# A GIN pass whose selection matrices move to GpSimd and whose edge layer becomes three split products

## The reference

```python
e = edge_attr @ W_edge + b_edge                       # 50,000 x 128 by 128 x 256
msg = jax.nn.relu(x[src] + e)
agg = jax.ops.segment_sum(msg, dst, num_segments=x.shape[0])
h = (1.0 + eps) * x + agg
h = jax.nn.relu(h @ W1 + b1) @ W2 + b2                # 256 x 256 each
h = relu((h - mean) * jax.lax.rsqrt(var + BN_EPS) * gamma + beta)
x = _layernorm(x + h, axis=-1)
```

## Time and profile before

| | us |
|---|---|
| median of 3 runs | 3568.29 |
| lowest to highest | 3567.71 to 3569.58 |
| profiled execution | 3571.73 |
| its span (first to last instruction) | 3570.0 |

### The profile page before, as it was taken

How to read it: one execution, slowest core, us unless ns; L and a number is a source line. 1 busy time by engine, 2 the same in 40 slices (tenths; PEclk the granted TensorE clock), 3 DMA queues, 4 the chain that set the end, 5 groups by cost and what they waited for, 6 DMA issues and landing times. The chain is left out here.

```text
span 3570.0 us, 89002 instructions
## 1 busy us (share of the span) xinstructions
PE 3158.8 (88%) x24644; PEld 3057.8 (86%) x24644; DVE 2807.0 (79%) x7960; ACT 2847.8 (80%) x5909; POOL 2230.7 (62%) x2320
## 2 busy tenths in 40 slices
PE   3999999999995444447999999899999979999998
PEld 2999999999995344437999999799999979999998
DVE  5999999999996777775666666466666659999997
ACT  1777777777774778786888888688888859999999
POOL 3655555555541666646777775677777657666663
PEclk8999999999997555558999999999999989999999
DMA  3666666666652999987878777688777769999996
GB/s 90 197 183 183 177 181 181 175 178 184 184 175 87 332 341 348 339 306 222 257 256 258 251 251 229 197 259 259 251 256 255 245 205 325 318 315 317 314 317 228
DMA packets 655160, 859.14 MB, mean 241 GB/s; under 512 B 131005, under 2 KB 516821, under 8 KB 655056
## 3 DMA queue, kind: packets, MB, share of 16 engines
q1 hardware_dynamic: 564778, 652.15, 56.7%
q0 software_dynamic: 87024, 205.39, 18.7%
q10 hardware_dynamic: 3254, 0.43, 0.1%
HBM read 632.57 MB, written 257.52 MB: 249 GB/s over the span
## 5 line engine op out<-in xcount | busy, mean ns | idle before, releaser
L530 POOL DMA_INDIRECT rows<-x_in,node_i x490 | 592.9, 1210 | 439.7 <-DVE raw L1097 283.1
L530 POOL DMA_INDIRECT rows<-gb_scratch,node_i x441 | 448.8, 1018 | 224.2 <-issue 111.9
L530 POOL DMA_INDIRECT rows<-x_scratch,node_i x441 | 449.0, 1018 | 186.1 <-issue 117.8
L530 POOL DMA_INDIRECT rows<-ga_scratch,node_i x441 | 448.9, 1018 | 185.2 <-issue 117.6
L1466 DVE TENSOR_TENSOR gcn_agg_lo<-gcn_agg_ps,gcn_agg_hi 128x1024 fp32r<-128x1024 f32 x196 | 240.0, 1224 | 380.1 <-ACT gcn_agg_hi L1508 380.1
L558 PE MATMUL gcn_agg_ps<-gcn_select,gcn_rows_hi 128*128 128x256 f32 (+2 forms) x1960 | 502.6, 290 | 18.7 <-DVE gcn_rows_lo L1476 18.7
L558 PE MATMUL gcn_agg_ps<-gcn_select,gcn_rows_lo 128*128 128x256 f32 (+2 forms) x1960 | 484.1, 287 | 0.0
L572 PE MATMUL gcn_h_ps<-g_hi,gcn_agg_hi 128*128 128x256 f32 x1568 | 450.6, 287 | 0.0
L572 PE MATMUL gcn_h_ps<-g_lo,gcn_agg_hi 128*128 128x256 f32 x1568 | 447.8, 286 | 0.0
L572 PE MATMUL gcn_h_ps<-g_hi,gcn_agg_lo 128*128 128x256 f32 x1568 | 445.3, 284 | 0.0
L1493 ACT ACTIVATE gcn_h<-gcn_h_ps,one_by_degree 128x256 f32<-128x256 f32 x784 | 308.0, 476 | 158.7 <-PE gcn_h_ps L572 158.5
(11 more groups left out here) (200 smaller groups left out, 11027.9 us busy)
## 6 DMA issues: line engine op xcount, KB each, us to landing
own<-x_t_in SPq DMA_DIRECT2D x196, 256.0 KB, 2.7
h_scratch<-h2t SPq DMA_DIRECT2D x196, 256.0 KB, 2.9
h2t_in<-h_scratch SPq DMA_DIRECT2D x98, 512.0 KB, 5.2
x_sb<-x_q_in SPq DMA_DIRECT2D x98, 512.0 KB, 7.0
x_scratch<-x SPq DMA_DIRECT2D x98, 512.0 KB, 5.6
gcn_own<-x_scratch SPq DMA_DIRECT2D x98, 512.0 KB, 4.5
ga_scratch<-gcn_h SPq DMA_DIRECT2D x98, 512.0 KB
gcn_own<-ga_scratch SPq DMA_DIRECT2D x98, 512.0 KB, 4.3
```

The lines of the kernel that those rows point to most:

```text
L530: pool.indirect_dma_start(out=c["rows"][:, slot, row_block(slot, b) if shared else b], out_offset=None, in_=source[:, :], in_offset=bass.I ...
```

## The change

GpSimd makes the selection matrices: after the gathers of a quad it makes those of two pairs, five places back, each waiting for the agg product of four pairs before; the ring of selections grows from two pairs to four. DVE's part for them goes. The edge layer becomes a split product: ACT rounds the attributes to attr_hi (lag 2, ahead of the bias copy), DVE subtracts to attr_lo (lag 2, last in its step), and PE multiplies three times per block in fp32r; PE waits for attr_split in place of the load. The weight w_edge is split in the constants like the other weights.

```diff
-SPLIT = ("w1", "w2", "g1", "g2", "g3")
+SPLIT = ("w_edge", "w1", "w2", "g1", "g2", "g3")
...
+        if beside is not None:
+            for q in range(2 * quad - 5, 2 * quad - 3):
+                if q >= 0:
+                    beside(q)
...
-def select_matrices(nc, c, pair, select):
-
-    for k, b in enumerate(range(*pair.blocks)):
+def select_pair(nc, c, q, select):
+
+    for k, b in enumerate(range(FIRST, BLOCKS) if q % 2 else range(FIRST)):
         first, end = SPAN[b]
-        last = nc.vector.tensor_scalar(select[:, k, 0:end - first], c["iota32"][:, first:end],
-                                       c["place"][:, bass.ds(pair.quad, 1), b], None, ALU.is_equal)
+        last = nc.gpsimd.tensor_scalar(select[:, k, 0:end - first], c["iota32"][:, first:end],
+                                       c["place"][:, q // 2, b:b + 1], None, ALU.is_equal)
     return last
...
+        attr_hi = m.sb("attr_hi", [P, 2, FIRST * P], F32R)
+        attr_lo = m.sb("attr_lo", [P, 2, FIRST * P], F32R)
...
-        select = m.sb("gin_select", [P, 2, FIRST, 320], F32R)
+        select = m.sb("gin_select", [P, RING, FIRST, 320], F32R)
...
-                gather_quads(nc, pool, c, dram["x"], gathered, rows_added, 2, table_steps)
+                def selections(q):
+
+                    if q >= RING:
+                        pool.wait_ge(agg_done, q - RING + 1)
+                    select_pair(nc, c, q, select[:, q % RING]).then_inc(select_done, 1)
+
+                gather_quads(nc, pool, c, dram["x"], gathered, rows_added, 2, table_steps, selections)
+                for q in range(2 * NQ - 5, NP):
+                    selections(q)
...
-                        pe.wait_ge(loaded[pair.place], pair.group_landed(pair.loads))
+                        pe.wait_ge(attr_split, pair.done())
                         pe.wait_ge(biased, pair.done())
+                        terms = products([attr_hi[:, b], attr_lo[:, b]], [c["w_edge_hi"], c["w_edge_lo"]])
                         for k in range(pair.new):
-                            last = nc.tensor.matmul(edge_ps[:, b, k], attr[:, pair.place, k * P:(k + 1) * P], c["w_edge"][:],
-                                                    start=False, stop=True, skip_group_check=True)
+                            for n, (a, w) in enumerate(terms):
+                                last = nc.tensor.matmul(edge_ps[:, b, k], a[:, k * P:(k + 1) * P], w[:],
+                                                        start=False, stop=n == len(terms) - 1,
+                                                        skip_group_check=True)
...
+                    if pair := at(2):
+                        b = pair.slot % 2
+                        act.wait_ge(loaded[pair.place], pair.group_landed(pair.loads))
+                        if pair.has(2):
+                            act.wait_ge(edge_done, pair.before(2))
+                        nc.scalar.copy(attr_hi[:, b, 0:pair.new * P], attr[:, pair.place, 0:pair.new * P]).then_inc(attr_rounded, 1)
...
-                    if pair := at(5):
-                        b, s = pair.slot % 2, pair.slot
-                        if pair.has(2):
-                            dve.wait_ge(agg_done, pair.before(2))
-                        select_matrices(nc, c, pair, select[:, b]).then_inc(select_done, 1)
...
+                    if pair := at(2):
+                        b = pair.slot % 2
+                        dve.wait_ge(attr_rounded, pair.done())
+                        if pair.has(2):
+                            dve.wait_ge(edge_done, pair.before(2))
+                        nc.vector.tensor_tensor(attr_lo[:, b, 0:pair.new * P], attr[:, pair.place, 0:pair.new * P],
+                                                attr_hi[:, b, 0:pair.new * P].bitcast(F32), ALU.subtract)\
+                            .then_inc(attr_split, 1)
...
-                keep[name + part] = m.sb(name + part, [P, 2, D], F32R)
+                keep[name + part] = m.sb(name + part, [P, D] if name == "w_edge" else [P, 2, D], F32R)
```

More of the change, by code:

```diff
@@ L513, in row_block, with gather_quads @@
     return (k + 1) % BLOCKS if slot == 0 else k
-def gather_quads(nc, pool, c, source, gathered, rows_free, per, tables=None):
+def gather_quads(nc, pool, c, source, gathered, rows_free, per, tables=None, beside=None):
     bound = pool.to_reg(NPAD - 1)
@@ L890, in gin_pass @@
         stored = [m.sem(f"gin_stored{s}") for s in range(RING)]
-        names = ("edge_done select_done rows_added msg_rounded "
+        names = ("attr_rounded attr_split edge_done select_done rows_added msg_rounded "
                  "msg_split biased agg_done h0_done h0_rounded h0_split h1_done h1_ready h1_split h2_done h2_ready stats_done")
-        (edge_done, select_done, rows_added, msg_rounded,
+        (attr_rounded, attr_split, edge_done, select_done, rows_added, msg_rounded,
          msg_split, biased, agg_done, h0_done, h0_rounded, h0_split, h1_done, h1_ready, h1_split, h2_done, h2_ready,
@@ L987, in step @@
                             pe.wait_ge(h0_done, pair.before(1))
-                        sum_into_columns(nc, pair, agg_ps, select[:, b], [msg_hi[:, half], msg_lo[:, half]]).then_inc(agg_done, 1)
+                        sum_into_columns(nc, pair, agg_ps, select[:, pair.slot], [msg_hi[:, half], msg_lo[:, half]]).then_inc(agg_done, 1)
                 pipeline(pe, step)
```

## The result

| | before | after |
|---|---|---|
| median, us | 3568.0 (3566.44 to 3569.58, 4 runs) | 3771.43 (3764.63 to 3778.76, 4 runs) |
| profiled execution, us | 3571.73 | 3765.63 |

The change makes the kernel slower: ratio 1.0569, 95% interval 1.0549 to 1.0589, some 203 us.

What follows compares the result with a forecast made beforehand. PE was taken to bound the kernel; after the change POOL, at 7.6 + 3.7 + 0.7 = 12.0 us per quad, makes the last agg product 134 us later: 3571.7 + 134 - 3.4 = 3702 us, range 3555 to 3850.

Steps and rivals of the forecast that it cites:

- The bound: GIN pass: POOL, at 12.0 us per quad, paces instead of PE at 10.4, through the selections' own length; chance 0.55.
- their waits: POOL's selections held up by DVE's two-input operations: 0.7 us per quad for five, bounds 0 to 1.5.
- The sum: POOL's 12.0 us per quad over 98 quads puts the last agg product at 1236 us, 134 later; 3702 us in all.
- gathers and issue: POOL's five gathers per quad, each 1.22 us plus 0.30 of issue: 7.6 us.
- selections' own length: Five selections per quad on POOL, without waits: 3.7 us, the middle of 2.3 and 5.1.
- The affine selection: POOL's float32 row pricing the selections' low end: 0.29 us for 128 columns, together 2.3 us for five.
- The one-input loop: The skill's rule for GpSimd, 512 elements in 769 ns: five selections would take 1.8 us; the prediction held the trace against it.
- Cheap selections: Rival: a selection with waits stays under 0.6 us, PE paces, 21 us come off before repayments: 3555 to 3570; chance 0.26.
- Both repayments: Costs set against the edge layer's 21 us gain: 8 to 10 us at the start, 0 to 13 at table steps.
- The shared read side: Rival: POOL and DVE hold each other up reading SBUF: 3643 us, or 3565 to 3590 if only DVE is held; chance 0.14.
- Switching: Rival: changing between gathers and selections costs POOL 2.0 us once or twice a quad: 3850 or above; chance 0.05.
- ACT and attr_hi at nothing: attr_hi adds some 1.0 us a quad to ACT, costing 0 while ACT keeps its 1.3 us idle.

Runs made afterwards that it cites:

- selections were made once: The changed kernel, but GpSimd makes only the first four pairs' selections, reused by all later pairs, PE waiting for all four groups at the start; 3588.91 us.
- the 3561.94: The changed kernel with the first four pairs' selections used throughout, attr_lo ahead of msg_lo, PE waiting at the start for its own pair alone; 3561.94 us, ratio 0.9986.
- the iotas: The changed kernel, but GpSimd writes 960 integers to scratch in place of each selection, the first two pairs' selections used throughout; 3713.65 us, ratio 1.0411.
- 3608.05: The changed kernel, but DVE makes the selections of even pairs and GpSimd only those of odd pairs; 3608.05 us, ratio 1.0109.
- 3574.8: The changed kernel with DVE selecting for even pairs, GpSimd for odd ones, and attr_lo moved ahead of msg_lo on DVE; 3574.8 us, ratio 1.0022.

## Why the prediction was right

The measured 3771 us lies 69 above the predicted 3702. The range, 3555 to 3850, held gains and losses alike, so the time alone says little; the bound and its terms do.

*The bound* was the one forecast: POOL, by the selections' length and their waits. Idle on raw is gone, PE is late at agg, and the last agg product moved by 199 us: nearly all of the 203 is lost where the sum put it. Busy over 90% was nearly so (89%; the 121 us of issue don't count as busy). PE's idle time came under other names than gin_select.

*The sum* gave a last agg at 1236 us; it came at 1301. Its terms:

| per quad, us | predicted | measured | from |
|---|---|---|---|
| gathers and issue | 7.6 | 7.5 | groups of after |
| selections' own length | 3.7 (2.3 to 5.1) | 4.4 | undisturbed ones |
| their waits | 0.7 (0 to 1.5) | 0.7 | mean less undisturbed |
| together | 12.0 | 12.6 | 800 us / 63.6 |

The mis-sized term is the selections' length, where the prediction took the middle of two rows. Undisturbed, 128 columns take 0.59 us (the least of all 490 selections), 256 take 0.91 and 320 take 1.07 (the least of their kinds; 2.88 above is two of the one and one of the other): 4.4 for the five. The row of the same operation, hot_node at 0.58, was exact for 128 columns, and only its growth with columns was overdrawn: 2.5 ns a column on top of 0.28, where the prediction had 3.8 on top of 0.10. The affine selection, which shared the element type, was no guide. The selections are 0.7 us longer, the gathers 0.1 shorter; a quad's 12.58 instead of 12.0 is 98 x 0.58 = 57 us of the 65. The other 8 are the end less the start: 57 + 98 x 12.58 = 1290 lies 11 us before the last agg product, which comes 15 after POOL's last selection (1286); and POOL's first gather comes 1 us earlier than before, and the first selections cost no 2 us more. 3571.7 + 198.9 - 3.4 = 3767 stands against the measured 3771.

*The one-input loop.* The Trainium skill (GPSIMD Engine Reference, Performance versus the Vector engine) gives 769 ns for 512 elements as the best case of a tight one-input loop, by which, an estimate, five selections take 1.8 us. The selections of this trace do not reach it: 4.4 us without waits, and 0.91 for 256 columns. Whether the operand that this comparison takes per partition is the reason, no run shows.

*Cheap selections* (the first rival) fell with that length: 4.4 is 0.88 each, over the 0.6 at which POOL decides. Its steps came true where selections were made once, 4.8 and 5.6 us. Its time did not: in the change's own order 3588.91, or near 3574 without that run's long first wait, against its 3555 to 3570 (the 3561.94 has attr_lo moved as well). Both repayments were larger than put. The step with a table is 0.68 late (some 0.5), 24 times 16 us against at most 13. And the second pair's agg starts 11.3 us later (8 to 10 predicted; 89.51 in the run of 3561.94 against 78.24), the seventh 14.0.

*The shared read side* happens, in the size of the forecast's term, not of the rival: it is the 0.7 a quad in the table, and the iotas show it from the other side. Between 100 and 1090 us, the 256 selections that overlap h1t_lo, h0t_lo, msg_lo and attr_lo by less than 0.02 us take 0.89 us on average, and the 82 that overlap them by over 0.3 us take 1.40; iotas take 0.93 and 0.94. That the sum agrees is in part luck: the prediction gave each selection 0.14, and the trace has 0.13 for each of 256 columns, 0.33 for that of 128 and nothing for that of 320. It also holds DVE: msg_lo of 768, 0.94 beside an iota, took 1.06 at 701.10, where a selection ended 0.12 after it began. DVE has time to spare here, so only POOL's side counts.

*Switching* fell: selections that follow a gather start within 0.1 us of it, and the gather behind them after 0.17.

*ACT and attr_hi at nothing*: right. ACT has the slack, and no row of after has PE wait for ACT's part of the edge layer. Where POOL and attr_lo are out of the way, PE waits 20.3 us for ACT in front of h1; how much of that is attr_hi's, no row tells.

## What to carry to other kernels

When work moves to an idle engine, add it up on that engine's own path per unit of work before counting what the old engine gains: POOL was busy 57% of the time, but 5.1 us more per quad took it past PE. Price an operation by a row of the same operation on that engine before one of the same element type (here hot_node was exact and the affine selection was not), and take apart its fixed part and its growth with columns. And where a new operation feeds the first instruction of another engine's step, its place in the order can decide: moving attr_lo alone took off 33 us (3608.05 to 3574.8), with the amount of work unchanged.

## What the runs showed that was not expected

On GpSimd this comparison costs nearly the same for 128 columns in float32 (0.593 us) as hot_node's for 16-bit (0.583): at this size, halving the bytes buys next to nothing.

Iotas, which only write, lengthen some of DVE's smallest operations. The mean of place (one tensor input, 20 columns) rises from 0.18 in the kernel before to 0.70 us beside them, and that of low from 0.24 to 0.64; raw_place, with two inputs, does not rise (0.19 before, 0.17 here). Before, then with the iotas, 200 to 1000 us:

```profile
L1055 DVE TENSOR_SCALAR low<-raw_place,fast 128x20 f32<-128x20 f32 x19 | 4.5, 235 | 0.7
...
L1072 DVE TENSOR_SCALAR place<-place_after 128x20 f32 x19 | 3.3, 176 | 0.0
```

```profile
L1102 DVE TENSOR_SCALAR place<-place_after 128x20 f32 x17 | 11.9, 697 | 0.0
...
L1085 DVE TENSOR_SCALAR low<-raw_place,fast 128x20 f32<-128x20 f32 x17 | 10.9, 641 | 0.6
...
L1082 DVE TENSOR_TENSOR raw_place<-window,quad_base 128x20 f32 x17 | 2.9, 171 | 0.0
```

The Trainium skill (SBUF — State Buffer, Who interferes with whom) has both halves: a DVE instruction with two SBUF inputs contends with a GpSimd instruction that reads SBUF and not with one that only writes, while a tensor_scalar in a 2-port mode takes the whole shared pair of ports. By that, the trace agrees; that these operations run in such a mode no row shows by itself.

PE's granted clock in the GIN pass fell from 1.00 to 0.95. Busy time and clock in pieces of 2 us:

```profile
724.00:726.00 2.00, 1.43 (x13) 1.23 (x11) 2.00 (x5) 0.91 (x3) 1.66 (x3) 1.00 0.97 324
726.00:728.00 2.00, 0.50 (x4) 0.53 (x5) 0.01 (x1) 2.00 (x6) 2.00 (x3) 0.98 0.42 139
728.00:730.00 2.00, 2.00 (x11) 2.00 (x11) 0.87 (x2) 0.74 (x2) 2.00 (x3) 0.50 0.00 0
730.00:732.00 2.00, 2.00 (x14) 2.00 (x13) 2.00 (x4) 1.22 (x2) 1.53 (x3) 0.67 0.38 101
732.00:734.00 2.00, 2.00 (x19) 2.00 (x19) 1.68 (x4) 0.29 (x2) 1.70 (x2) 1.00 0.80 196
```

PE idles in front of agg, busy 1.43 and then 0.50 of 2 us; then, busy again, it is granted 0.50, the level of 1.2 GHz, and 1.00, that of 2.4 GHz, again from 732. At 0.50 its 256-column products follow at 0.21 us (729.22 to 731.13), where 0.12 is usual. Such a wait of PE thus costs more than its own length. Here POOL set the pace, so no run shows what that part came to in the end.
